# Scores, maxima and masks issued as four products of 32 columns of the array

## The chip, the cores and the metric

The kernel runs on one core of a Trainium2 chip. The metric is device time in microseconds (us) of one execution, lower is better. The engines are named as in the profile: PE is TensorE's products and PEld its weight loads, DVE is VectorE, ACT is ScalarE, POOL is GpSimd, SP is SyncE, which issues DMA transfers.

## The reference

The input is one sequence of 4096 tokens with 256 channels. Four blocks follow one another, each on a layer norm and with a residual sum: a gated recurrence, a feed-forward layer, causal attention with 16 heads of 16 channels, and the feed-forward layer again.

```python
# gated recurrence
i, f, o = (sigmoid(x @ W + b) for W, b in ...); s = tanh(x @ Ws + bs)
h_t = f_t * h_{t-1} + i_t * s_t
y = layernorm(x + o * h) * gamma + beta
# feed-forward
xr = mu_r * x + (1 - mu_r) * x_prev; xk = mu_k * x + (1 - mu_k) * x_prev
out = sigmoid(xr @ W_r.T) * (relu(xk @ W_k.T) ** 2 @ W_v.T)
# attention, in chunks of queries
scores = einsum('bhqd,bhkd->bhqk', q, k) * scale      # -inf where key > query
p = softmax(scores - max(scores)); oc = einsum('bhqk,bhkd->bhqd', p, v)
out = oc @ Wo.T + bo
```

## The kernel before

The layers run in 16 units of 256 tokens. Attention runs in 32 steps: 8 chunks of 512 queries, and for each 4 groups of 4 heads. The heads of a group lie in two pairs. Of each pair one head has rows 0 to 63 of the array and the other rows 64 to 127, `row = HALF * half`, so that two products can run at once, one in each half of the rows. Queries and keys are kept in f16, each in two parts that stand one under the other, and make a stack of 48 rows (`SCORE_ROWS`), or 50 (`STACK`) with two rows that hold the shift by the maximum.

Per step TensorE does this. A maximum ("max", L1751) is a product of up to 512 keys for 128 queries, f16, 48 rows; where its keys reach the diagonal, two products of 64 columns follow in the same half (L1758), bf16, which add the mask. VectorE reduces each to a column (L1539) and frees its PSUM bank. Once a step's maxima are known, VectorE and TensorE form the shift (L1766, f16) and a DMA puts it under the queries. Scores ("scores", L1783) are products of 128 keys for up to 512 queries, f16, 50 rows. ScalarE takes the exponential out of the bank (L1283, or L1294 for two banks at once). P V ("pv", L1804) is four f32 products, one per head, each with 128 rows and 17 columns of the array, side by side in the four groups of 32 columns. Its result is transposed (L1813) and divided.

The layers' products (L1600 in `channels_out`, L1608 in `tokens_out`) are f32 with 128 rows. Each is already issued as four products of 32 columns:

```python
for c in range(0, P, COLUMNS):
    ins = nc.tensor.matmul(bank_chan(b)[c:c + COLUMNS, e], ...
```

Transposes (L1593, L1647, L1813) use all 128 rows and 128 columns.

The order of the work of all engines is written down ahead by `schedule()`, a planner that has costs for each piece of work. It knows three ways in which the array is divided, "half" for maxima, masks and scores, "pv" for P V and the layers' products, "full" for transposes, and counts `SWITCH = 95` ns from one to another. What it gives, `ORDER`, is followed by all engines. Seven PSUM banks go round between maxima, scores and the layers' work, the eighth is P V's. Before TensorE writes a bank again, `claim` waits for the bank's last reader: `span_reduced` for a maximum, `exp_done` for scores.

Of the kernel before, what the change touches and what calls it, by code (L numbers as in the profile page):

```python
# [15 lines left out]
P = 128  # L16
# [23 lines left out]
PAIRS = HG // 2  # L40
# [13 lines left out]
Q_RING = 4  # L54
# [590 lines left out]
def build(nc, x, Wi, bi, Wf, bf, Wo_gate, bo_gate, Ws, bs, gamma, beta, WqT, bq, WkT, bk, WvT, bv, WoT, bo,  # L645
          WrT, WkfT, WvfT, mu_r, mu_k, out):
    with ExitStack() as ctx:
# [95 lines left out]
        def bank(n):  # L743
            return psum[:, n * CHUNK:(n + 1) * CHUNK]
# [836 lines left out]
        def _(pe):  # L1581
# [34 lines left out]
            for op in ORDER:  # L1616
# [69 lines left out]
                elif name in ("q", "kk"):  # L1686
                    _, u, e, b = op
                    if e == 0:
                        claim(b, *((whole_ready[name], u - EARLY + 1) if parts_late(u) else
                                   (part1_ready[name], u + 1)))  # L1690
                        if u == 0:
                            pe.wait_ge(qk_scaled, 1)
                        pe.wait_ge(x3T_ready, u + 1)
                    ins = channels_out(b, weights["aq" if name == "q" else "ak"], a_x3T, e)
                    if e == 1:
                        ins.then_inc(full[name], 1)
                elif name == "v":
                    _, u, j, b = op
                    if j == 0:
                        claim(b, v_ready, u + 1)  # L1700
                        pe.wait_ge(x3T_ready, u + 1)
                    ins = tokens_out(b, weights["av"], a_x3T, j)
                    if j == 1:
                        ins.then_inc(full["v"], 1)
                elif name == "aT":
                    _, u, b = op
                    claim(b, aT_ready, u + 1)
                    pe.wait_ge(attn_ready, GROUPS * (u // 2 + 1))
                    to_channels(b, attn[:, u % 2 * UT:(u % 2 + 1) * UT, :]).then_inc(full["aT"], 1)
                elif name == "proj":  # L1710
                    _, u, j, b = op
                    if j == 0:
                        claim(b, x3_copied if u < UNITS - LATE else x3_ready, u + 1)
                        pe.wait_ge(aT_ready, u + 1)
                    ins = tokens_out(b, weights["ao"], c_columns(u), j)
                    if j == 1:
                        ins.then_inc(full["proj"], 1)
                elif name == "bound":
                    b = op[1]
                    claim(b, bound_read, 1)  # L1720
                    pe.wait_ge(filled, FILLS)
                    pe.wait_ge(prepared, 1)
                    for w in range(2):
                        for k in range(CT):
                            ins = nc.tensor.matmul(bank_tok(b)[:, w], ones, w_squared[:, w, k],
                                                   start=(k == 0), stop=(k == CT - 1))
                    ins.then_inc(full["bound"], 1)
                elif name == "bo":
                    b = op[1]
                    claim(b, bo_ready, 1)  # L1730
                    for k in range(CT):
                        ins = nc.tensor.matmul(bank(b)[:, 0:DIM], bv_cols[:, k], weights["ao"][:, k],
                                               start=(k == 0), stop=(k == CT - 1))
                    ins.then_inc(full["bo"], 1)
                elif name == "max":
                    _, m, half, b = op
                    s, qt, u, k0, k1 = MAXIMA[m]
                    g, c = STEPS[s]
                    maxed += 1
                    claim(b, span_reduced, maxed)  # L1740
                    if s not in q_seen:
                        q_seen.add(s)
                        pe.wait_ge(q_loaded[s % Q_RING], 16 * 2 * len(Q_PARTS) * (s // Q_RING + 1))
                    if c not in k_seen:
                        k_seen.add(c)
                        pe.wait_ge(k_loaded[c % 2], 16 * 2 * len(K_PARTS) * (c // 2 + 1))
                        if c == 0:
                            pe.wait_ge(consts_ready, 4)
                    row = HALF * half
                    ends = k1 == (c * TT + qt + 1) * P  # L1750
                    ins = nc.tensor.matmul(bank(b)[:, 0:k1 - k0],  # L1751
                                           q_stack[row:row + SCORE_ROWS, s % Q_RING, u, qt * P:(qt + 1) * P],
                                           k_stack[row:row + SCORE_ROWS, g * PAIRS + u, k0:k1],
                                           start=True, stop=not ends)
                    if ends:
                        for n in range(2):
                            k = k1 - P - k0 + n * HALF
                            ins = nc.tensor.matmul(bank(b)[:, k:k + HALF], mask_rows[row:row + HALF, n],  # L1758
                                                   mask_keys[row:row + HALF], start=False, stop=(n == 1))
                    ins.then_inc(m_full[half], 1)  # L1760
                elif name == "shift":
                    _, s, b = op
                    claim(b, shift_copied, s + 1)
                    pe.wait_ge(shift_ready, s + 1)
                    for qt in range(TT):
                        ins = nc.tensor.matmul(  # L1766
                            bank(b)[0:HG * MAX_ROWS, qt * P:(qt + 1) * P],
                            shift_parts[:, s % 2, qt * HG:(qt + 1) * HG, :].rearrange("p h r -> p (h r)"),
                            ident_h[:], start=True, stop=True)
                    ins.then_inc(full["shift"], 1)  # L1770
                elif name == "scores":
                    _, tile, i, b = op
                    s, j = TILES[tile]
                    g, c = STEPS[s]
                    q0 = max(0, j - c * TT) * P
                    row, u = HALF * (i % 2), i // 2
                    if j == 0 and scores == HG * tile:
                        pe.wait_ge(shift_placed[s % 2], 16 * HG * (s // 2 + 1))
                        if s == 0:
                            pe.wait_ge(unit_placed, 16 * 2)  # L1780
                    scores += 1
                    claim(b, exp_done, scores)
                    nc.tensor.matmul(bank(b)[:, q0:], k_stack[row:row + STACK, g * PAIRS + u, j * P:(j + 1) * P],  # L1783
                                     q_stack[row:row + STACK, s % Q_RING, u, q0:], start=True, stop=True)\
                        .then_inc(scored[i % 2], 1)
                elif name == "pv":
                    tile = op[1]
                    s, j = TILES[tile]
                    g, c = STEPS[s]
                    d = j - c * TT  # L1790
                    if d >= 0:
                        pe.wait_ge(masked, s * TT + d + 1)
                    else:
                        pe.wait_ge(exp_done, HG * (tile + 1))
                    if j == 0:
                        if s == 0:
                            pe.wait_ge(pv_cleared, 1)
                        else:
                            pe.wait_ge(o_copied, s)
                    if d == 0 and g == 0:  # L1800
                        pe.wait_ge(v_ready, 2 * (c + 1))
                    q0 = max(0, d) * P
                    for h in range(HG):
                        ins = nc.tensor.matmul(pv_bank[32 * h:32 * h + VW, q0:], v_aug[:, j, g * HG + h, :],  # L1804
                                               probs[:, tile % PROBS, h, q0:], start=(j == 0),
                                               stop=(j == TT * (c + 1) - 1))
                    ins.then_inc(pv_done, 1)
                elif name == "out":
                    _, s, b = op
                    claim(b, attn_ready, s + 1)  # L1810
                    pe.wait_ge(o_copied, s + 1)
                    for qt in range(TT):
                        ins = nc.tensor.transpose(bank(b)[:, qt * P:(qt + 1) * P], oT[:, qt * P:(qt + 1) * P],  # L1813
                                                  ident[:])
                    ins.then_inc(full["out"], 1)
# [28 lines left out]
```

## Time and profile before

| | |
|---|---|
| time, median of 2 runs | 1751.32 us |
| the two runs | 1751.12 and 1751.53 us |
| span of the profiled execution | 1749.5 us |
| products on TensorE (as many loads) | 18242 |
| TensorE busy with products | 1709.4 us |
| VectorE busy | 1509.9 us |
| ScalarE busy | 1342.8 us |
| GpSimd busy | 688.8 us |

Both runs lie within 0.5 us of each other; the span of the profiled execution is what the instructions cover, 1.8 us less than the median. A product is booked from its start to its modelled end in PSUM, so that the times of products that follow one another overlap. A weight load (PEld) stands apart from the products that it serves. TensorE's share of busy time therefore says little of short pauses; they are read from the starts.

### The profile page before, as it was taken

The numbers are of one execution on the slowest core, as the hardware profiler recorded it, in microseconds if no ns is written. First come the engines' busy times: TensorE is split into PE (matmuls) and PEld (weight loads), VectorE is DVE, ScalarE is ACT, GpSimd is POOL, SyncE is SP. The second block draws the span as 40 slices with busy tenths as digits, with TensorE's granted clock in tenths as the row PEclk, the third lists the DMA queues.
The fourth block names the chain that finished last, engine by engine and source line by source line (L and its number), as shares of the span: only waits on it lengthen the run. The fifth ranks groups of instructions, "written<-read, shape, count | busy, mean of one in ns | idle before, by whom it ended". The sixth has DMA issues, their size and how long they took to land.

```text
span 1749.5 us, 45658 instructions
## 1 busy us (share of the span) xinstructions
PE 1709.4 (98%) x18242; PEld 641.3 (37%) x18242; DVE 1509.9 (86%) x2975; ACT 1342.8 (77%) x2781; POOL 688.8 (39%) x994
## 2 busy tenths in 40 slices
PE   8999999999999999999999999999999999999997
PEld 6554444344433333334333333332332322222324
DVE  6778979986899999998998999999999999999802
ACT  3336677767677878876888879889889899898894
POOL 3348666478562453428336225220311220212201
PEclk9999999999999999999999999999999999999999
DMA  4132021003002000020000020000002000000000
GB/s 113 56 74 57 27 46 31 18 21 62 28 18 48 13 30 13 8 48 25 6 24 8 21 29 6 24 13 2 7 14 34 18 4 3 14 1 14 2 7 13
DMA packets 57000, 43.71 MB, mean 25 GB/s; under 512 B 8788, under 2 KB 56788, under 8 KB 56788
## 3 DMA queue, kind: packets, MB, share of 16 engines
q1 hardware_dynamic: 54548, 39.75, 9.4%
q8 instruction: 144, 2.36, 0.6%
q10 hardware_dynamic: 2240, 1.05, 0.5%
q14 instruction: 68, 0.56, 0.1%
HBM read 24.00 MB, written 16.25 MB: 23 GB/s over the span
## 4 chain that ended last, share of the span: by engine, by line
PE 60%; DVE 13%; ACT 4%; issue 2%; POOL 2%; SPq 0%; DMA 0%; ACTq 0%; POOLq 0%; DVEq 0%
PE psum L1804 21%; PE psum L1783 12%; PE psum L1751 12%; DVE span_max L1539 12%; PE psum L1608 7%; PE psum L1600 6%; ACT probs L1283 2%; ACT probs L1294 1%; PE psum L1593 1%; PE psum L1813 1%; PE psum L1758 1%; DVE rows L1478 0%; DVE shift_parts L1554 0%; POOL rows L1100 0%; DVE small L1388 0%
## 5 line engine op out<-in xcount | busy, mean ns | idle before, releaser
L1539 DVE TENSOR_REDUCE span_max<-psum 128x1 f32<-128x512 f32 (+3 forms) x2304 | 1313.7, 636 | 98.6 <-PE psum L1751 73.8
L1283 ACT ACTIVATE probs<-psum 128x512 f32<-128x512 f32 (+3 forms) x2148 | 1040.7, 570 | 173.3 <-PE psum L1783 170.1
L1804 PE MATMUL psum<-probs,v_aug 128*17 128x512 f32 (+3 forms) x4608 | 564.9, 562 | 1.3 <-ACT oT L1303 0.8
L1751 PE MATMUL psum<-k_stack,q_stack 48*128 48x512 f16 (+3 forms) x2304 | 533.2, 363 | 4.4 <-DVE span_max L1539 2.7
L1783 PE MATMUL psum<-q_stack,k_stack 50*128 50x512 f16 (+3 forms) x2304 | 521.0, 364 | 5.5 <-DVE span_max L1539 0.7
L1783 PEld LDWEIGHTS psum<-q_stack,k_stack 50*128 50x128 f16 x2304 | 148.7, 93 | 388.7 <-ACT probs L1283 272.4
L1751 PEld LDWEIGHTS psum<-k_stack,q_stack 48*128 48x128 f16 x2304 | 156.0, 93 | 287.9 <-DVE span_max L1539 214.3
L1149 POOL TENSOR_SCALAR_AFFINE_SELECT probs<-probs 128x512 f32<-128x512 f32 x128 | 81.1, 637 | 254.3 <-ACT probs L1283 209.7
L1804 PEld LDWEIGHTS psum<-probs,v_aug 128*17 128x17 f32 x4608 | 77.7, 95 | 136.4 <-issue 114.7
L1188 ACT ACTIVATE rows<-psum,cols 128x256 f32<-128x256 f32 x128 | 53.9, 479 | 56.0 <-PE psum L1600 52.6
L1758 PE MATMUL psum<-mask_keys,mask_rows 64*128 64x64 bf16 x1024 | 93.5, 189 | 0.0
L1142 POOL TENSOR_TENSOR rows<-rows 128x512 f32<-128x512 f32 x26 | 33.1, 1273 | 152.1 <-ACT rows L1225 152.1
L1758 PEld LDWEIGHTS psum<-mask_keys,mask_rows 64*128 64x128 bf16 x1024 | 76.4, 95 | 27.3
L1294 ACT ACTIVATE probs<-psum 128x1024 f32<-128x1024 f32 (+3 forms) x78 | 70.9, 1241 | 3.9 <-PE psum L1783 3.9
L1600 PE MATMUL psum<-rows,w_k 128*32 128x256 f32 x1024 | 68.3, 383 | 3.7 <-DVE rows L1505 2.6
L987 POOL TENSOR_SCALAR rows<-rows,small 128x256 f32<-128x256 f32 x124 | 67.9, 555 | 6.8
L1090 POOL TENSOR_TENSOR rows<-rows 128x512 f32<-128x512 f32 x26 | 27.1, 1041 | 109.9 <-ACT rows L1202 109.9
L1566 DVE RECIPROCAL inv_sum<-psum 128x16 f32<-128x16 f32 x32 | 8.1, 253 | 71.6 <-PE psum L1813 70.9
L1608 PE MATMUL psum<-w_r,rows 128*32 128x256 f32 x1024 | 67.9, 383 | 1.0 <-ACT probs L1283 0.2
L1137 POOL TENSOR_SCALAR rows<-rows 128x512 f32<-128x512 f32 x26 | 16.4, 630 | 131.0 <-ACT rows L1209 130.9
L1388 DVE BATCH_NORM_STATS2 small<-rows 128x6 f32<-128x256 f32 x160 | 59.3, 413 | 9.9 <-POOL rows L1048 3.9
L1608 PE MATMUL psum<-w_v,rows 128*32 128x256 f32 x1024 | 67.4, 383 | 0.4 <-DVE span_max L1539 0.2
(139 smaller groups left out, 1548.1 us busy)
## 6 DMA issues: line engine op xcount, KB each, us to landing
q_stack<-q_parts SPq DMA_DIRECT2D x192, 32.0 KB, 2.0
k_stack<-k_parts SPq DMA_DIRECT2D x42, 128.0 KB, 5.0
rows<-in_x SPq DMA_DIRECT2D x16, 256.0 KB, 2.7
q_parts<-rows SPq DMA_DIRECT2D x32, 128.0 KB, 2.0
k_parts<-rows SPq DMA_DIRECT2D x32, 128.0 KB, 2.0
out<-rows SPq DMA_DIRECT2D x16, 256.0 KB, 2.2
x_rows<-rows SPq DMA_DIRECT2D x14, 256.0 KB, 2.2
rows<-x_rows SPq DMA_DIRECT2D x14, 256.0 KB, 2.7
```

The costliest lines, as they stand in the source:

```text
L987: ins = nc.gpsimd.tensor_scalar(dst[:, j], src[:, j], neg_mean[:, ln, j:j + 1], rstd[:, ln, j:j + 1], ALU.add, ALU.mult)
L1149: nc.gpsimd.affine_select(out=tri, in_=tri, compare_op=ALU.is_ge, fill=0.0, base=0, pattern=[[0, HG], [1, P]], channel_multiplier=-1).then ...
L1283: act.activation(probs[:, tile % PROBS, i, q0:], bank(b)[:, q0:], ACT.Exp, scale=SCALE / QK_SCALE).then_inc(exp_done, 1)
L1294: act.activation(probs[:, tile % PROBS, i:i + 2, q0:], psum[:, b * CHUNK:(b + 2) * CHUNK].rearrange("p (h q) -> p h q", h=2)[:, :, q0:], A ...
L1388: ins = nc.vector.bn_stats(stats[:, ln, j], src[:, j])
L1539: nc.vector.tensor_reduce(span_max[:, s % SPAN_RING, row:row + 1, k0 // SPAN:k0 // SPAN + 1], bank(b)[:, 0:k1 - k0], AX.X, ALU.max).then_i ...
L1600: ins = nc.tensor.matmul(bank_chan(b)[c:c + COLUMNS, e], w[:, k, e * P + c:e * P + c + COLUMNS], src[:, k], start=(k == 0), stop=(k == CT ...
L1608: ins = nc.tensor.matmul(bank_tok(b)[c:c + COLUMNS, j], src[:, k, j * P + c:j * P + c + COLUMNS], w[:, k], start=(k == 0), stop=(k == CT - 1))
L1751: ins = nc.tensor.matmul(bank(b)[:, 0:k1 - k0], q_stack[row:row + SCORE_ROWS, s % Q_RING, u, qt * P:(qt + 1) * P], k_stack[row:row + SCORE ...
L1758: ins = nc.tensor.matmul(bank(b)[:, k:k + HALF], mask_rows[row:row + HALF, n], mask_keys[row:row + HALF], start=False, stop=(n == 1))
L1783: nc.tensor.matmul(bank(b)[:, q0:], k_stack[row:row + STACK, g * PAIRS + u, j * P:(j + 1) * P], q_stack[row:row + STACK, s % Q_RING, u, q0 ...
L1804: ins = nc.tensor.matmul(pv_bank[32 * h:32 * h + VW, q0:], v_aug[:, j, g * HG + h, :], probs[:, tile % PROBS, h, q0:], start=(j == 0), sto ...
```

## The change

Each product of a maximum, of a mask and of scores is issued as four, each for 32 columns of the array and 32 partitions of the bank. Rows, moving operands and results are the same. The wait for the bank stands ahead of the first of the four, and the semaphore is raised by the last. The planner is not touched, so that the order of all work stays.

```diff
-                    ins = nc.tensor.matmul(bank(b)[:, 0:k1 - k0],
-                                           q_stack[row:row + SCORE_ROWS, s % Q_RING, u, qt * P:(qt + 1) * P],
-                                           k_stack[row:row + SCORE_ROWS, g * PAIRS + u, k0:k1],
-                                           start=True, stop=not ends)
+                    for w in range(0, P, COLUMNS):
+                        ins = nc.tensor.matmul(bank(b)[w:w + COLUMNS, 0:k1 - k0],
+                                               q_stack[row:row + SCORE_ROWS, s % Q_RING, u,
+                                                       qt * P + w:qt * P + w + COLUMNS],
+                                               k_stack[row:row + SCORE_ROWS, g * PAIRS + u, k0:k1],
+                                               start=True, stop=not ends)
                     if ends:
                         for n in range(2):
                             k = k1 - P - k0 + n * HALF
-                            ins = nc.tensor.matmul(bank(b)[:, k:k + HALF], mask_rows[row:row + HALF, n],
-                                                   mask_keys[row:row + HALF], start=False, stop=(n == 1))
+                            for w in range(0, P, COLUMNS):
+                                ins = nc.tensor.matmul(bank(b)[w:w + COLUMNS, k:k + HALF],
+                                                       mask_rows[row:row + HALF, n, w:w + COLUMNS],
+                                                       mask_keys[row:row + HALF], start=False, stop=(n == 1))
                     ins.then_inc(m_full[half], 1)
...
-                    nc.tensor.matmul(bank(b)[:, q0:], k_stack[row:row + STACK, g * PAIRS + u, j * P:(j + 1) * P],
-                                     q_stack[row:row + STACK, s % Q_RING, u, q0:], start=True, stop=True)\
-                        .then_inc(scored[i % 2], 1)
+                    for w in range(0, P, COLUMNS):
+                        ins = nc.tensor.matmul(bank(b)[w:w + COLUMNS, q0:],
+                                               k_stack[row:row + STACK, g * PAIRS + u, j * P + w:j * P + w + COLUMNS],
+                                               q_stack[row:row + STACK, s % Q_RING, u, q0:], start=True, stop=True)
+                    ins.then_inc(scored[i % 2], 1)
```

Two places on TensorE show it in the row of instructions. The first is a stretch of maxima (L1751, in the changed kernel L1752), masks (L1758, then L1761) and scores (L1783, then L1788) between two tiles of P V (L1804, then L1810). The shape is columns of the array by columns of the moving operand. Before:

```order
L1804 MATMUL psum<-probs,v_aug 17x512 x4
L1751 MATMUL psum<-k_stack,q_stack 128x512
L1783 MATMUL psum<-q_stack,k_stack 128x512
L1751 MATMUL psum<-k_stack,q_stack 128x256
L1758 MATMUL psum<-mask_keys,mask_rows 128x64 x2
L1751 MATMUL psum<-k_stack,q_stack 128x256
L1758 MATMUL psum<-mask_keys,mask_rows 128x64 x2
L1783 MATMUL psum<-q_stack,k_stack 128x512 x3
L1804 MATMUL psum<-probs,v_aug 17x512 x4
```

The same place after:

```order
L1810 MATMUL psum<-probs,v_aug 17x512 x4
L1752 MATMUL psum<-k_stack,q_stack 32x512 x4
L1788 MATMUL psum<-q_stack,k_stack 32x512 x4
L1752 MATMUL psum<-k_stack,q_stack 32x256 x4
L1761 MATMUL psum<-mask_keys,mask_rows 32x64 x8
L1752 MATMUL psum<-k_stack,q_stack 32x256 x4
L1761 MATMUL psum<-mask_keys,mask_rows 32x64 x8
L1788 MATMUL psum<-q_stack,k_stack 32x512 x12
L1810 MATMUL psum<-probs,v_aug 17x512 x4
```

Nothing changes its place; each row has four times the instructions. The other place is a set of transposes (L1813, then L1819), which takes the array whole, between P V and scores. Before:

```order
L1804 MATMUL psum<-probs,v_aug 17x512 x4
L1813 MATMUL psum<-ident,oT 128x128 x4
L1783 MATMUL psum<-q_stack,k_stack 128x512
L1751 MATMUL psum<-k_stack,q_stack 128x512
L1783 MATMUL psum<-q_stack,k_stack 128x512 x2
```

And after:

```order
L1810 MATMUL psum<-probs,v_aug 17x512 x4
L1819 MATMUL psum<-ident,oT 128x128 x4
L1788 MATMUL psum<-q_stack,k_stack 32x512 x4
L1752 MATMUL psum<-k_stack,q_stack 32x512 x4
L1788 MATMUL psum<-q_stack,k_stack 32x512 x8
```

Between transposes and scores the columns now change with the rows, as they did before between P V and scores. TensorE's products go from 18242 to 35138; the rows of VectorE, ScalarE and SyncE are the same, and so are those of GpSimd but for line numbers.

## Rows read from the trace of the kernel before

**Rows 1.** The page: span, and each engine's busy us (share) and instructions.

```profile
span 1749.5 us, 45658 instructions
...
PE 1709.4 (98%) x18242; PEld 641.3 (37%) x18242; DVE 1509.9 (86%) x2975; ACT 1342.8 (77%) x2781; POOL 688.8 (39%) x994
```

**Rows 2.** Windows of 200 us: length, then each engine's busy us, clock, DMA.

```profile
core 0: us, PE busy (x) PEld busy (x) DVE busy (x) ACT busy (x) POOL busy (x), PEclk, DMA share, GB/s
0.00:200.00 200.00, 186.96 (x2700) 110.64 (x2704) 153.15 (x402) 87.58 (x206) 107.26 (x178) 1.00 0.29 70
200.00:400.00 200.00, 197.74 (x2409) 83.00 (x2403) 165.42 (x352) 143.48 (x321) 127.25 (x184) 1.00 0.12 31
400.00:600.00 200.00, 195.90 (x2206) 76.68 (x2204) 177.90 (x350) 145.59 (x313) 111.77 (x155) 1.00 0.15 31
600.00:800.00 200.00, 198.66 (x2067) 70.34 (x2067) 186.96 (x356) 161.46 (x343) 88.49 (x127) 1.00 0.10 24
800.00:1000.00 200.00, 198.78 (x2122) 71.67 (x2116) 183.22 (x349) 160.25 (x338) 92.75 (x132) 1.00 0.05 16
1000.00:1200.00 200.00, 198.62 (x1903) 64.11 (x1897) 191.60 (x352) 169.72 (x353) 58.66 (x79) 1.00 0.08 17
1200.00:1400.00 200.00, 198.28 (x1853) 60.82 (x1849) 191.82 (x346) 176.47 (x362) 44.37 (x60) 1.00 0.08 16
1400.00:1600.00 200.00, 198.13 (x1731) 58.87 (x1729) 192.39 (x347) 181.09 (x372) 34.19 (x48) 1.00 0.02 6
1600.00:1749.50 149.50, 136.32 (x1285) 45.15 (x1281) 67.39 (x127) 117.19 (x179) 24.10 (x35) 1.00 0.03 8
```

**Rows 3.** The chain of waits, by line, share of the span.

```profile
by line: PE psum L1804 20.6%; PE psum L1783 12.0%; PE psum L1751 11.7%; DVE span_max L1539 11.6%; PE psum L1608 6.7%; PE psum L1600 5.8%; issue 2.4%; ACT probs L1283 2.0%; ACT probs L1294 1.4%; PE psum L1593 1.3%; PE psum L1813 0.7%; PE psu
```

**Rows 4.** Groups by form: count | busy us, mean ns | idle before, releaser.

```profile
L1758 PE MATMUL psum<-mask_keys,mask_rows 64*128 64x64 bf16 x1024 | 93.5, 189 | 0.0
...
L1751 PE MATMUL psum<-k_stack,q_stack 48*128 48x384 f16 x128 | 33.2, 327 | 0.3 <-ACT probs L1283 0.2
...
L1783 PE MATMUL psum<-q_stack,k_stack 50*128 50x384 f16 x128 | 30.5, 328 | 0.5 <-DVE span_max L1539 0.3
...
L1751 PE MATMUL psum<-k_stack,q_stack 48*128 48x256 f16 x128 | 28.8, 275 | 0.4 <-DVE span_max L1539 0.2
...
L1751 PE MATMUL psum<-k_stack,q_stack 48*128 48x128 f16 x128 | 24.0, 222 | 0.5 <-DVE span_max L1539 0.4
```

**Rows 5.** Four lines in short windows: count, duration in ns min/median/max, starts.

```profile
L1608 PE MATMUL psum<-w_r,rows x16: 379/379/403, 1203.0 to 1203.7; 128*32 128x256 f32 x16
...
L1804 PE MATMUL psum<-probs,v_aug x8: 592/598/604, 1207.3 to 1207.7; 128*17 128x512 f32 x8
...
L1751 PE MATMUL psum<-k_stack,q_stack x2: 387/387/387, 1210.2 to 1210.2; 48*128 48x512 f16 x2
...
L1783 PE MATMUL psum<-q_stack,k_stack x3: 376/377/378, 1210.5 to 1210.9; 50*128 50x512 f16 x3
```

**Rows 6.** Timeline of TensorE, 1203 to 1208 us: start us, us, instruction, count.

```profile
1203.03 1.07 PE L1608 MATMUL psum<-w_r,rows 128*32 128x256 f32 x16
1203.91 0.39 PE L1766 MATMUL psum<-ident_h,shift_parts 128*8 128x128 f16 x4
...
1206.05 0.39 PE L1783 MATMUL psum<-q_stack,k_stack 50*128 50x512 f16 x1
1206.05 0.39 PE L1751 MATMUL psum<-k_stack,q_stack 48*128 48x512 f16 x1
1206.54 0.39 PE L1783 MATMUL psum<-q_stack,k_stack 50*128 50x512 f16 x2
1206.76 0.38 PE L1751 MATMUL psum<-k_stack,q_stack 48*128 48x512 f16 x2
1206.98 0.38 PE L1783 MATMUL psum<-q_stack,k_stack 50*128 50x512 f16 x1
1207.29 1.05 PE L1804 MATMUL psum<-probs,v_aug 128*17 128x512 f32 x8
1208.27 0.39 PE L1751 MATMUL psum<-k_stack,q_stack 48*128 48x512 f16 x1
1208.28 0.39 PE L1783 MATMUL psum<-q_stack,k_stack 50*128 50x512 f16 x1
```

**Rows 7.** Timeline of TensorE about two sets of transposes at 649 us.

```profile
648.74 0.66 PE L1813 MATMUL psum<-ident,oT 128*128 128x128 f32 x4
649.23 0.60 PE L1593 MATMUL psum<-ident,rows 128*128 128x128 f32 x4
649.76 0.39 PE L1783 MATMUL psum<-q_stack,k_stack 50*128 50x512 f16 x2
```

**Rows 8.** Timeline: eight weight loads of P V, and four products of L1608.

```profile
1207.29 0.13 PEld L1804 LDWEIGHTS psum<-probs,v_aug 128*17 128x17 f32 x8 [0.43 <-ACT probs L1283]
...
1203.03 0.42 PE L1608 MATMUL psum<-w_r,rows 128*32 128x256 f32 x4
```

## The prediction

> **What bounds the kernel now.** I read the first part of the page, then the busy time of each engine by stretches of 200 us, then the costliest groups, and last the timeline of TensorE. The page gives TensorE 98% of the span, and the granted clock is 1.00, the 2.4 GHz level, in every stretch [rows 1, 2]. But VectorE stands at 183 to 192 us of every 200 from 600 to 1600 us and ScalarE at 160 to 181 [rows 2], and the chain of waits runs 11.6% of the span through the reduction of the maxima [rows 3]. So TensorE leads, with VectorE close behind it in that part.
>
> TensorE's 98% must be read with care. A product of 512 columns of f16 is booked with 377 to 387 ns [rows 5], but two of them, one in each half of the rows, start every 0.22 us: 1206.54, 1206.76, 1206.98 [rows 6]. So 0.16 us of each booking is the tail of the pipeline, and a pause shorter than the tail looks busy. Two kinds of pause hide there. One is a wait for a bank: a pair starts at 1206.05 and the next only at 1206.54 [rows 6]. The other is the switch between ways in which the array is divided. The product at 1206.98 should be through its columns at 1207.20, and P V starts at 1207.29. P V then streams two sets of four products. One set streams for 0.43 us (1.05 us for the eight, less the 0.60 of a single product [rows 5] and 0.02 by which the four of a set start apart), so the columns are through near 1208.17, and the next scores start at 1208.27. Each switch costs some 0.095 us in which nothing streams. Where the division stays, no such gap is there: sixteen products of L1608 at 1203.03 and the four of L1766 at 1203.91 stand 0.88 us apart, which is four sets of 0.216 and the first load [rows 6].
>
> How many switches there are I counted in TensorE's order of instructions: 801 stretches of scores, maxima and masks, 752 entered from P V or a layer's product and 766 left to one; the rest border on transposes. That is 1,518 switches, 144 us, the largest sum that the change could touch.
>
> **The change part by part. The switch.** After the change both sides use 32 columns of the array, but scores still use half the rows and P V all of them. What the trace must answer is whether a change of rows alone costs the gap. It has such a place: a transpose uses all 128 rows and 128 columns, a score half the rows and 128 columns. Eight transposes start at 648.74 and 649.23; the first four take 0.49 us to the next four (4 x 0.107, the rate at which P V streams, plus the first load), the second four 0.53 us to the scores at 649.76, although no load of a transpose lies in this second time [rows 7]. So the change of rows alone shows 0.10 us. I found the same in all places after transposes. I therefore keep the whole 144 us: gain 0. The other bound is the full 144 us, since a transpose may differ from a product in more than its rows; it is rival one. The Trainium skill (TensorEngine Tiling, "Key Properties") says that a change of tiling mode drains TensorE, and lists 64x32 and 128x32 as two modes; by it too nothing is saved here.
>
> **The steady stream.** A pair of 512 columns becomes eight products and eight loads per 0.22 us. Issue isn't the limit: eight loads with the first four products between them go out in 0.13 us less the 0.093 of one load, or 3 to 4 ns an instruction [rows 8], and sixteen need some 55 ns. Nor should the reading be: P V already streams four f32 operands side by side, and four tiles of f16 at twice the columns per us in each half of the rows ask the same bytes of each partition. I take 0, with an upper bound of twice the time (the f32 rate, 0.43 us) in rival two.
>
> **The first load of a stretch.** The first pair after a switch is booked with 387 ns and the later ones with 377: 10 ns of load show. For 128x32 f32 it is 403 against 379, 24 ns; for 128x17 604 against 592, 12 ns [rows 5]. A load of 32 columns is nearest to the 24: + 14 ns for each of 801 stretches, 11 us. Bounds 0 (as the 17 columns) and 41 ns (both halves' loads in turn), 0 to 33 us. The skill ("Gotcha 2: Feature Incompatibilities" on the same page) says that column tiling excludes the fast weight load, which agrees in sign; no run here shows yet that the wide load is a fast one.
>
> **The stagger.** This is the main term. The two products of a pair start within 10 ns. Four narrow ones start 6.7 ns apart: four of L1608 take 0.42 us where one takes 0.403 [rows 5, 8]. Eight then start over 47 ns, and each tile keeps its lag to the end of the stretch, where the switch waits for the last. By my count 479 stretches have an even number of products and end on both halves: + 43 ns; 322 end on one half: + 20 ns. That is 20.6 + 6.4 = 27 us. If products go out at 3.5 ns, it is 13 us. The skill (TensorE: Matmul & The Clock Gate, "The mechanism" in Part 3) gives some 4 ns per tile; by it the term would be 15 us.
>
> **The masks.** 1,024 products of 64 columns stand in 512 groups of two, each now eight. Eight at 6.7 ns are 54 ns, as long as two of 64 columns stream, so one half loses little; the other half's next product waits behind them in order, some 20 ns, in about half of the groups: 5 us, bounds 0 and 20 us.
>
> TensorE's own sum is 11 + 27 + 5 = 43 us, bounds 13 to 85 us.
>
> **How much of it reaches the end.** The order of work is unchanged on all engines. Where TensorE waits for a bank, as at 1206.54, a later TensorE only shortens the wait. At 192 us of 200, VectorE has 8 us of slack per 200 us and TensorE's term is 5 us per 200 us; where the chain runs over VectorE it costs little, elsewhere all. I take six tenths: 26 us. Bounds three tenths of the low sum, 4 us, and all of 43. The profiled execution spans 1749.5 us and the runs took 1751.1 and 1751.5 [rows 1], 1.8 outside it, which stays. Forecast: 1751.3 + 26 = 1777 us, own range 1755 to 1800.
>
> **The rivals.** One: rows don't count, only columns, and the switch to P V is free. For it: no place in the trace changes rows between two real products. Against it: 0.10 us at every change from transposes to scores. TensorE would give back 144 us, 16 us of each 200, but VectorE and ScalarE don't follow. Taking 184 us for the first three stretches, VectorE's busy time with 2% on top for the next five (191, 187, 195, 196, 196) and 137 for the last gives 1,654 [rows 2]; the time would be some 1,660 us, range 1,630 to 1,700.
>
> Two, on the slow side: the narrow loads don't run side by side across the two halves but go in turn. Loads of 27 ns (the 24 ns above) in turn for eight tiles are 0.21 us, just hidden behind 512 columns; from there down they bind. The first pair of each stretch would pay 0.2 us x 801 = 160 us, the narrower products 41 us (L1751 has 128, or 64 pairs, of each of 128, 256 and 384 columns and L1783 as many [rows 4]; 128 pairs each at 0.16, 0.11 and 0.05 us), the 256 pairs of masked products 0.32 us each, 82 us: about 280 us, at nine tenths 2,000 us. In a milder form only the two halves take turns: 27 ns more per stretch, 22 us, and 27 ns more for each of the 1,024 masks, 28 us, which with the 43 makes 93 us on TensorE and at nine tenths 1,835 us. Four loads of a layer's set clearly don't go in turn, since they share the 24 ns; for eight nothing is shown. Half-rate streaming would be worse, 0.22 us x 2,304, over 2,200 us.
>
> Three: the waits take up everything, 1,752 us.
>
> **How the numbers follow.** Forecast 0.60, rival one 0.17, rival two in its milder form 0.10 and in the others 0.05, rival three 0.08. Two per cent, about what a measurement tells from no change, is 35 us: up to 1786. Some three tenths of the forecast's case lies above it. So faster 0.17; slower 0.18 + 0.15 = 0.33; same 0.50. The range leaves out the worst forms of rival two and half of rival one, some 14 in 100 together: 1660 to 1840 us.
>
> **What the profile after would show.** A switch that stays: the last product of a stretch to the first of P V, and back, still 0.09 to 0.10 us after the columns are through, and no load of P V before it. Rival one shows loads of P V inside the stretch of scores. The stagger: eight starts over some 47 ns, and a lag of the same size at the end. The first load: first products booked some 24 ns longer than later ones; rival two shows eight starts or second pairs far later than 0.22 us. VectorE's busy time unchanged. The prediction is wrong if a stretch of three pairs, now 0.8 us from switch to switch, is shorter, or longer by over 0.1 us.

## The result, and the profile after

The changed kernel takes 1765.09 us (1764.61 and 1765.56), against 1751.32 us before: the ratio is 1.0079, with a 95% interval of 1.0049 to 1.0108. It is 13.8 us slower, inside what was forecast and on that side, but about half as much.

The page of the changed kernel, with the queue that fetches instructions:

```profile
span 1763.8 us, 79450 instructions
...
PE 1725.8 (98%) x35138; PEld 676.4 (38%) x35138; DVE 1512.2 (86%) x2975; ACT 1345.0 (76%) x2781; POOL 690.9 (39%) x994
...
q8 instruction: 276, 4.52, 1.1%
```

The span is 14.3 us longer than in [rows 1]. TensorE has 35138 products in place of 18242, VectorE and ScalarE work as long as before, and the fetch of instructions, 2.36 MB before and 4.52 after, holds 0.6% of the transfer engines before and 1.1% after.

The timeline of TensorE at the place of [rows 6], now at 1217 us (start us, us, instruction, count):

```profile
1216.61 0.40 PE L1788 MATMUL psum<-q_stack,k_stack 50*32 50x512 f16 x4
1216.62 0.40 PE L1752 MATMUL psum<-k_stack,q_stack 48*32 48x512 f16 x4
1217.10 0.41 PE L1788 MATMUL psum<-q_stack,k_stack 50*32 50x512 f16 x8
1217.33 0.40 PE L1752 MATMUL psum<-k_stack,q_stack 48*32 48x512 f16 x8
1217.55 0.39 PE L1788 MATMUL psum<-q_stack,k_stack 50*32 50x512 f16 x4
1217.86 1.05 PE L1810 MATMUL psum<-probs,v_aug 128*17 128x512 f32 x8
1218.84 0.40 PE L1752 MATMUL psum<-k_stack,q_stack 48*32 48x512 f16 x4
1218.86 0.40 PE L1788 MATMUL psum<-q_stack,k_stack 50*32 50x512 f16 x4
```

Pairs of four and four still start every 0.22 us: 1217.10, 1217.33, 1217.55. The stream is no slower with eight products in the place of two. Four take 0.40 us where one is booked with 0.387, and eight 0.41: they start some 3.3 ns apart, not 6.7. From the last scores, through their columns at 1217.77, to P V at 1217.86 it is 0.09 us, and from P V back to the maxima 0.98 us as before. So the switch is as dear as it was.

The same two sets of transposes as in [rows 7], in the changed kernel:

```profile
654.92 0.66 PE L1819 MATMUL psum<-ident,oT 128*128 128x128 f32 x4
655.41 0.60 PE L1593 MATMUL psum<-ident,rows 128*128 128x128 f32 x4
655.94 0.41 PE L1788 MATMUL psum<-q_stack,k_stack 50*32 50x512 f16 x8
```

0.49 and 0.53 us, as in [rows 7]. Over the whole trace the gap from the columns' end to the next product is, in the median, 94 ns from scores to P V or a layer, before and after, and 96 ns the other way, where it was 98. In these 752 places a wide product of f16 starts in the median 4 ns after its load and a narrow one 2 ns, which is most of the difference.

The first products after a switch (count, duration in ns min/median/max):

```profile
L1752 PE MATMUL psum<-k_stack,q_stack x4: 386/386/387, 1216.6 to 1216.6; 48*32 48x512 f16 x4
```

They are booked with 386 to 387 ns, as the wide ones are in [rows 5]. The narrow load of f16 shows no more than the wide one.

Two windows of 200 us (length, then PE, PEld, DVE, ACT, POOL busy, clock):

```profile
core 0: us, PE busy (x) PEld busy (x) DVE busy (x) ACT busy (x) POOL busy (x), PEclk, DMA share, GB/s
...
200.00:400.00 200.00, 198.49 (x4464) 86.63 (x4458) 166.80 (x357) 142.02 (x317) 126.18 (x184) 1.00 0.13 31
...
1200.00:1400.00 200.00, 198.41 (x4044) 63.72 (x4028) 190.34 (x344) 175.34 (x359) 42.01 (x58) 1.00 0.08 15
```

VectorE does the same work in more time: it is busy for 190.34 us of these 200, where [rows 2] have 191.82.

Both traces hold the same 1740 stretches between changes of division in the same order, so that they can be laid side by side. From the starts of the products (f16 at 2.4 columns per ns and f32 at 1.2) I summed each kind. The 801 stretches of scores, maxima and masks take 577.2 us before and 595.7 after, 18.5 more. All other stretches change by 0.8 us. The gaps between stretches take 196.3 and 191.5 us, 4.8 less, of which 3 ns x 801 = 2.4 us is the earlier start and the rest shorter waits. An even stretch without masks is longer by 19 ns in the median (285 of them), an odd one by 11 ns (204), an even one with four masks by 23 ns (104). The prediction's own sign of being wrong was a stretch of three pairs that is shorter, or longer by over 0.1 us: the 162 stretches of three full pairs without masks go from 0.663 to 0.683 us in the median, counted from the first start to the end of the columns.

### The profile page after: what moved, and what is told of

Its sections match the earlier page's. It is cut to its first block, busy times and chain, and to the rows that moved or that the text cites. A ratio compares the mean times of both kernels' runs of the same rounds, so it can differ in the third digit from the quotient of the medians.

```text
span 1763.8 us, 79450 instructions
## 1 busy us (share of the span) xinstructions
PE 1725.8 (98%) x35138; PEld 676.4 (38%) x35138; DVE 1512.2 (86%) x2975; ACT 1345.0 (76%) x2781; POOL 690.9 (39%) x994
## 3 DMA queue, kind: packets, MB, share of 16 engines
q8 instruction: 276, 4.52, 1.1%
## 4 chain that ended last, share of the span: by engine, by line
PE 74%; DVE 14%; ACT 4%; POOL 3%; issue 3%; DMA 0%; SPq 0%; ACTq 0%; POOLq 0%; DVEq 0%
PE psum L1810 23%; PE psum L1788 14%; PE psum L1752 14%; DVE span_max L1539 11%; PE psum L1600 9%; PE psum L1608 9%; ACT probs L1283 2%; PE psum L1593 2%; ACT probs L1294 1%; PE psum L1761 1%; PE psum L1819 1%; DVE rows L1478 1%; POOL small L981 0%; POOL rows L987 0%; DVE small L1388 0%
## 5 line engine op out<-in xcount | busy, mean ns | idle before, releaser
L1283 ACT ACTIVATE probs<-psum 128x512 f32<-128x512 f32 (+3 forms) x2148 | 1042.6, 567 | 185.2 <-PE psum L1788 181.9
L1810 PE MATMUL psum<-probs,v_aug 128*17 128x512 f32 (+3 forms) x4608 | 565.0, 562 | 1.3 <-ACT oT L1303 0.8
L1752 PE MATMUL psum<-k_stack,q_stack 48*32 48x512 f16 (+3 forms) x9216 | 548.0, 363 | 3.4 <-DVE span_max L1539 2.4
L1788 PE MATMUL psum<-q_stack,k_stack 50*32 50x512 f16 (+3 forms) x9216 | 536.2, 364 | 5.2 <-DVE span_max L1539 1.0
L1788 PEld LDWEIGHTS psum<-q_stack,k_stack 50*32 50x32 f16 x9216 | 167.2, 89 | 383.0 <-ACT probs L1283 269.4
L1752 PEld LDWEIGHTS psum<-k_stack,q_stack 48*32 48x32 f16 x9216 | 175.5, 89 | 278.1 <-DVE span_max L1539 207.3
L1810 PEld LDWEIGHTS psum<-probs,v_aug 128*17 128x17 f32 x4608 | 77.8, 95 | 138.7 <-issue 115.9
L1761 PE MATMUL psum<-mask_keys,mask_rows 64*32 64x64 bf16 x4096 | 99.0, 189 | 0.2 <-issue 0.2
L1761 PEld LDWEIGHTS psum<-mask_keys,mask_rows 64*32 64x32 bf16 x4096 | 84.9, 94 | 19.9 <-issue 0.3
L1608 PE MATMUL psum<-w_r,rows 128*32 128x256 f32 x1024 | 68.1, 383 | 1.7 <-issue 0.8
L1608 PE MATMUL psum<-w_v,rows 128*32 128x256 f32 x1024 | 67.7, 383 | 0.4 <-DVE span_max L1539 0.2
```

The lines of the kernel that those rows point to most:

```text
L1283: act.activation(probs[:, tile % PROBS, i, q0:], bank(b)[:, q0:], ACT.Exp, scale=SCALE / QK_SCALE).then_inc(exp_done, 1)
L1608: ins = nc.tensor.matmul(bank_tok(b)[c:c + COLUMNS, j], src[:, k, j * P + c:j * P + c + COLUMNS], w[:, k], start=(k == 0), stop=(k == CT - 1))
L1752: ins = nc.tensor.matmul(bank(b)[w:w + COLUMNS, 0:k1 - k0], q_stack[row:row + SCORE_ROWS, s % Q_RING, u, qt * P + w:qt * P + w + COLUMNS], ...
L1761: ins = nc.tensor.matmul(bank(b)[w:w + COLUMNS, k:k + HALF], mask_rows[row:row + HALF, n, w:w + COLUMNS], mask_keys[row:row + HALF], start ...
L1788: ins = nc.tensor.matmul(bank(b)[w:w + COLUMNS, q0:], k_stack[row:row + STACK, g * PAIRS + u, j * P + w:j * P + w + COLUMNS], q_stack[row: ...
```

## The experiments

### One and two: does the gap come with rows, with columns, or with the kind of work?

Only half of the keys of each tile enter P V in these two, so that it takes 64 rows. In the first, all of scores and P V then divide the array alike; in the second (on the kernel before), only the columns differ. Half of P V's sum is left out.

```diff
-  pv_bank[32 * h:32 * h + VW, q0:], v_aug[:, j, g * HG + h, :], probs[:, tile % PROBS, h, q0:]
+  pv_bank[32 * h:32 * h + VW, q0:], v_aug[0:HALF, j, g * HG + h, :], probs[0:HALF, tile % PROBS, h, q0:]
```

> The changed kernel, in which P V's products take only the first 64 of the 128 keys of each tile (rows 0 to 63 of the array, 32 columns), so that half of P V's sum is left out. Scores, maxima, masks and P V then all use 64 rows and 32 columns. Theory (the gap comes with any change in the rows or the columns that a product divides the array into): no gap between scores and P V, and loads of P V inside the stretch of scores; the gaps between P V and the layers' products, which had none, are new. Changes of division fall from 1740 to 753, 987 x 0.095 = 94 us less on TensorE; VectorE holds part of it back: 1,670 to 1,700 us. Rival (the gap comes with any change between f16 and f32 work, or between scores and P V as such): the gap of 0.09 us stays, 1,755 to 1,765 us.

Measured: 1736.8 us, ratio to the kernel before 0.9927 (0.9904 to 0.995), 28 us under the changed kernel. Timeline of TensorE, and below it of the loads:

```profile
1202.07 0.57 PE L1752 MATMUL psum<-k_stack,q_stack 48*32 48x512 f16 x8
1202.28 0.39 PE L1788 MATMUL psum<-q_stack,k_stack 50*32 50x512 f16 x4
1202.50 1.03 PE L1810 MATMUL psum<-probs,v_aug 64*17 64x512 f32 x8
1203.11 0.40 PE L1788 MATMUL psum<-q_stack,k_stack 50*32 50x512 f16 x4
```

```profile
1202.28 0.32 PEld L1810 LDWEIGHTS psum<-probs,v_aug 64*17 64x17 f32 x8
```

P V starts at 1202.50, 0.22 us after the last scores, which is their stream and nothing else, and its loads go out at 1202.28, while those scores run. At 1203.11 scores run in the other half beside P V. In the 747 passages from scores to P V, P V begins in the median 10 ns before all columns of the scores are through, and in eight of ten at most 3 ns after. At the passages from P V to a layer's product, where there was no gap, there is one now, 92 ns in the median (58 of them); both sides are f32 there, and only the rows differ. So it is the division, and neither f16 against f32 nor the kind of work. The time lies above the 1,670 to 1,700 us that I expected. The window of 1200 to 1400 us and the shares of the chain of waits, from the page, point to the reason:

```profile
1200.00:1400.00 200.00, 195.72 (x4116) 73.44 (x4112) 193.51 (x352) 178.14 (x367) 50.02 (x71) 1.00 0.08 18
```

```profile
PE 35%; DVE 30%; ACT 10%; issue 4%; POOL 3%; SPq 0%; DMA 0%; ACTq 0%; POOLq 0%; DVEq 0%
```

VectorE has 193.5 us of 200 and ScalarE 178, and 28% of the span in the chain is the reduction of the maxima, which was 11.6% in [rows 3]. What TensorE gained they didn't follow. A small part is the granted clock, whose mean was 0.988 to 0.996 in the three runs: if TensorE works all the time and the clock is either full or half, a mean of 0.996 costs 0.004 of the span, an estimate of 7 us.

> The kernel before, with the same half of P V's sum left out: scores with 64 rows and 128 columns, P V with 64 rows and 32 columns. Only the columns change between them. Theory (rows or columns): the gap stays, 1802 changes of division in place of 1740, 1,750 to 1,760 us. Rival (rows alone make the gap): as the run before it, under 1,700 us.

Measured: 1774.53 us in the median of five runs, the fastest 1756.95; ratio 1.0098 (1.0059 to 1.0136). Timeline:

```profile
1211.13 0.38 PE L1751 MATMUL psum<-k_stack,q_stack 48*128 48x512 f16 x2
1211.44 1.05 PE L1804 MATMUL psum<-probs,v_aug 64*17 64x512 f32 x8
1212.42 0.39 PE L1783 MATMUL psum<-q_stack,k_stack 50*128 50x512 f16 x1
```

1211.13 + 0.21 to 1211.44: the gap of 0.09 us stays, and back it is 95 ns in the median of 488. Columns alone make it too. The time is over what was expected, for another reason: the granted clock fell in some stretches (see the last section). I ran it again:

> The second experiment's kernel again, since its profiled run fell to a lower granted clock in one stretch. Theory as there: the gap stays, 1,750 to 1,760 us at the full clock.

Measured: 1768.55 us (1760.64 to 1778.46), ratio 1.0103 (1.0063 to 1.0144); the profiled execution, with a mean clock of 0.994, spans 1758.9 us. Above the range again, and with the full clock it was not seen. By the estimate used for experiment one the lost clock is 5 to 32 us in the nine executions of this kernel, and the time without it is 1,747 to 1,753 us in all of them, about that of the kernel before. That the gap stays doesn't hang on the time; it is read from the starts.

### Three: two products of 64 columns

```diff
-                    for w in range(0, P, COLUMNS):
+                    for w in range(0, P, HALF):
```

and in each of the three places slices `w:w + HALF`.

> Scores, maxima and masks as two products of 64 columns. Theory (the added time is the stagger, 3.3 ns for each product after the first, and the order of the masks): 4 starts over 10 ns at the end of an even stretch in place of 23 ns, some 5 us over the kernel before, 1,755 to 1,758 us. Rival (the time comes with the change of the form of the products or of their loads, not with their number): as the changed kernel, 1,765 us. If a load takes its columns at the narrow rate, the first products are booked with 400 ns in place of 387, and 13 ns x 801 = 10 us come on top: 1,766 us.

Measured: 1759.65 us, ratio 1.0046 (1.0033 to 1.006), 8.3 us over the kernel before. The first products after a switch:

```profile
L1752 PE MATMUL psum<-k_stack,q_stack x4: 400/400/400, 1209.5 to 1209.5; 48*64 48x512 f16 x4
```

400 ns in place of 387. So a load of 64 columns shows 13 ns more than one of 32, and also 13 more than the wide one of 128. Half of the expectation fails: the stagger is smaller than in the changed kernel, and the load, which I had put beside it with a question mark, is there. The two don't add to the 1,766 that I wrote: the stagger was only some 3 to 6 ns per stretch, so that the median stretch without masks is 17 to 20 ns longer, 13 of it the load. All 801 stretches together are 10.8 us longer (577.2 to 588.0), less than the medians would give, and the gaps are 1.9 us shorter. Why the sum falls short of the medians I didn't find out.

### Four and five: P V in two halves of the rows, in full

> The kernel before with six PSUM banks in rotation in place of seven and two buffers for rows of x in place of three, for which the planner makes another order. The control for the next run. More waits for banks: 1,760 to 1,800 us.

```diff
-BANKS, PV_BANK = 7, 7
+BANKS, PV_BANK = 6, 7
-X_ROWS = 3
+X_ROWS = 2
```

Measured: 1906.65 us, ratio 1.0888 (1.0871 to 1.0904). Far over what I expected: a bank and a buffer less, and the other order that the planner makes for them, cost 155 us. Which of the two it is was not separated.

> The whole computation, with the banks and buffers of the control. Scores, maxima and masks as in the changed kernel; P V as eight products, four heads with the first 64 keys into one bank and four with the last 64 keys into another, so that all of them use 64 rows and 32 columns. ScalarE copies both banks (some 0.5 us more per step, 16 us), and TensorE adds the two with products with the identity in place of the transposes (128 more of 0.107 us, 14 us). Theory: P V streams as long as before, since both halves run at once, and the gaps between scores and P V go: some 90 us less on TensorE, 14 more, and VectorE holds part of it back, so 40 to 70 us under the control. Rival (the sixteen f32 operands that P V now reads for two halves at once, or the two banks, slow its stream, or VectorE takes all): no less than the control.

```diff
+                    for n in range(2):
+                        rows = slice(HALF * n, HALF * (n + 1))
                         for h in range(HG):
-                            ins = nc.tensor.matmul(pv_bank[32 * h:32 * h + VW, q0:], v_aug[:, j, g * HG + h, :],
+                            ins = nc.tensor.matmul(bank(PV_BANK + n)[32 * h:32 * h + VW, q0:],
+                                                   v_aug[rows, j, g * HG + h, :], ...
```

Measured: 1932.05 us, ratio 1.1039 (1.1021 to 1.1058), 25 us over its control. The rival came true, though not by the means that it named. Timeline:

```profile
1200.82 0.40 PE L1789 MATMUL psum<-q_stack,k_stack 50*32 50x512 f16 x4
1201.04 1.04 PE L1813 MATMUL psum<-probs,v_aug 64*17 64x512 f32 x16
1202.03 0.40 PE L1789 MATMUL psum<-q_stack,k_stack 50*32 50x512 f16 x4
```

Sixteen products of two tiles of P V follow the scores after 0.22 us without a gap and take 1.04 us, as eight did: both halves stream at the full rate. The gap is gone, and the time with it isn't. The shares of the chain of waits, from the page:

```profile
PE 32%; DVE 28%; ACT 8%; POOL 3%; issue 3%; DMA 1%; ACTq 0%; POOLq 0%; DVEq 0%
```

27% of the span in the chain is VectorE's reduction of the maxima, 11% in the control, although VectorE is busy for only 1506 of 1930 us. Before a maximum TensorE sits idle for such a reduction 104 times and 24.0 us in all, against 39 times and 10.6 us in the control, so waits for banks took up at least part of what the gaps gave back. How the 25 us over the control come about I didn't isolate; the other copy by ScalarE and the added products are in it too.

### Six to eight: VectorE made light

VectorE reduces half the columns, so that its part in the 13.8 us, and in what experiment one gained, can be seen. The maximum is then taken over half the keys only.

```diff
-                                            bank(b)[:, 0:k1 - k0], AX.X, ALU.max).then_inc(span_reduced, 1)
+                                            bank(b)[:, 0:(k1 - k0) // 2], AX.X, ALU.max).then_inc(span_reduced, 1)
```

> The kernel before, in which VectorE reduces only the first half of the columns of each maximum, so that the maximum is over half the keys; VectorE's busy time falls by some 600 us. The base for the next two. TensorE's waits for VectorE go: 1,715 to 1,745 us.

Measured: 1726.55 us, ratio 0.9859 (0.9844 to 0.9874).

> The changed kernel with the same half reductions. Theory (TensorE's own term is 16 to 18 us, of which VectorE's waits took a few): 15 to 19 us above the base. Rival (the waits took nothing, and the 13.8 us are all that TensorE loses): 13 to 14 us above the base. Second rival (the added time comes in part by way of VectorE, since its banks come full later): 10 us or less above the base.

Measured: 1741.99 us, ratio 0.995 (0.9933 to 0.9967), 15.4 us over its base. I take that as TensorE's own term. It is 1.6 us over the 13.8, no more than the runs of one kernel lie apart here (1740.6 to 1743.0), so the times alone don't show that waits had swallowed something. The starts of the one profiled execution of each point to it: the stretches of scores are again 18.5 us longer (561.3 to 579.8), but the gaps only 2.9 us shorter, not 4.8.

> The first experiment's kernel (changed kernel, P V over the first 64 of 128 keys) with the same half reductions. Theory (the 987 gaps that are gone are worth 94 us to TensorE, and VectorE was what held them back): 80 us or more under the kernel of the run before it. Rival (ScalarE or the fixed order holds it back as much): within 50 us of it.

Measured: 1680.39 us, ratio 0.9599 (0.9584 to 0.9613), 61.6 us under the run before it. It lies between the theory's 80 and the rival's 50. Window of 1400 to 1600 us:

```profile
1400.00:1600.00 200.00, 195.03 (x4076) 72.14 (x4072) 116.92 (x334) 184.78 (x365) 39.15 (x52) 0.98 0.03 8
```

VectorE is out of the way with 117 us, and ScalarE stands at 185 of 200 in its place. The shares of the chain of waits, from the page:

```profile
PE 59%; ACT 22%; POOL 8%; issue 6%; DVE 2%; DMA 0%; ACTq 0%; POOLq 0%; DVEq 0%
```

The exponentials of ScalarE (L1283) hold 18% of the span, 2.0% in [rows 3]. The mean granted clock of 0.994 to 0.997 takes 5 to 10 us by the estimate used above. With VectorE as it is the same edit gained 28 us, so VectorE held back some 33 us of the 94; some 7 are the clock, and for the other 25 ScalarE and the fixed order are left. I didn't take these two apart.

### Nine and ten: without the masks

```diff
-                    ends = k1 == (c * TT + qt + 1) * P
+                    ends = False
```

> The kernel before without the masks' products (the maxima then see keys past the diagonal). Base for the next: 1,735 to 1,750 us.

Measured: 1746.29 us, ratio 0.9971 (0.996 to 0.9982).

> The changed kernel without the masks' products. Theory (stagger 12 us on TensorE, masks 6): 9 to 12 us above the base, in place of 13.8 with masks. Rival (the masks cost nothing, all is the stagger of the stretches): 13 to 15 us above the base.

Measured: 1754.5 us, ratio 1.0019 (1.001 to 1.0028), 8.2 us over its base, a little under the range of the theory and far from the rival's. By the starts the stretches are 12.4 us longer (568.0 to 580.4) and the gaps 4.5 us shorter. With masks it was 18.5 us: the masks carry 6 us, the stagger 12. This also speaks against a rival that I had not named, the fetch of twice the instructions (2.23 and 4.00 MB in these two): the stagger, worked out from the starts in the next section, is 12.3 us of the 12.4, and little is left for the fetch. With the masks in, nothing was added outside the stretches either.

## Why the prediction was right, and where its sizes were off

**The switch.** Kept at its full 144 us, from the transposes alone. The changed kernel shows it at every passage, experiment one shows it gone once rows and columns agree, and experiment two shows it with the columns alone different. The doubt that a transpose might differ in more than its rows can be dropped. Rival one was false. The Trainium skill (TensorEngine Tiling, "Key Properties") says that a change of tiling mode drains TensorE; the traces agree, with medians of 0.090 to 0.098 us for each change where nothing else is waited for.

**The steady stream.** Taken at 0, measured 0: 0.22 us per pair.

**The first load.** Taken at 14 ns, 11 us in all; it is 0 for 32 columns. The step that failed is the choice of the nearest row: I took 32 columns of f32 as nearest (24 ns). In f16 32 columns show 10 ns (387 less 377) and 64 columns 23 (400 less 377), so columns of f16 show about half the time of those of f32. The range held it, with 0 as its lower end. By the terms of the prediction the upper bound of TensorE's sum is 33 + 27 + 20 = 80 us, not the 85 written there; nothing hangs on it.

**The stagger.** Taken at 6.7 ns per product and 27 us in all; it is 3.3 ns and 12 us. 7 x 3.3 - 4 = 19 ns for even stretches and 3 x 3.3 = 10 for odd ones are what the medians show (19 and 11), and 479 x 0.019 + 322 x 0.010 = 12.3 us. The mistake is the same as with the load: I read the 6.7 ns from products of f32 and used it for f16. It is not the number of rows. P V of experiment two has 64 rows as the scores do, is f32, and follows a switch; four of its products take 0.62 us where one is booked with 0.600, and their starts lie 6.7 ns apart in the median of all its 572 tiles. What is left between them and the scores in these rows is the type of the elements:

```profile
1211.44 0.62 PE L1804 MATMUL psum<-probs,v_aug 64*17 64x512 f32 x4
...
L1804 PE MATMUL psum<-probs,v_aug x4: 600/600/602, 1211.4 to 1211.5; 64*17 64x512 f32 x4
```

The 3.5 ns that I gave as the lower bound was the better value. The Trainium skill (TensorE: Matmul & The Clock Gate, "The mechanism") gives some 4 ns per tile, which was nearer than my row.

**The masks.** Taken at 5 us, shown as 6 on TensorE by the two runs without them.

**What reaches the end.** Taken at six tenths. TensorE's own term with a light VectorE is 15.4 us and 13.8 us arrive, nine tenths. So the slack that I read out of VectorE's 183 to 192 us of 200 took up little. 43 x 0.6 = 26 was forecast. By the starts 18.5 us in the stretches of scores and 0.8 in the others, less 4.8 in the gaps, is 14.5 us, and the spans lie 14.3 apart. The two errors, one of size upward and one of passage downward, partly cancelled, which was luck: the 43 us at nine tenths would have been 39, nearly three times what was measured.

**The rivals.** Two (loads in turn) is excluded by the steady 0.22 us and by the first products' 387 ns. Three (all absorbed) is excluded by the interval.

## What to carry to other kernels

Before equalizing how two kinds of work divide TensorE's array, look whether rows and columns both agree afterwards: each change of either cost 0.09 to 0.10 us here, and a change that equalizes one of the two saves nothing. When a cost is read from the nearest row, take one with the same type of element before one with the same shape: both terms that were mis-sized here came from rows of f32. Splitting a product over groups of columns is nearly free in steady state, but it lengthens each stretch by the lag between first and last start; count the stretches, not the products. And where the gap can be removed, ask first whether the next engine, here VectorE at over 90%, can follow.

## What the runs showed that I had not expected

The granted clock fell with TensorE at work. Windows of experiment two, before, during and after (length, then PE, PEld, DVE, ACT, POOL busy, clock):

```profile
1020.00:1027.00 7.00, 6.56 (x79) 2.42 (x72) 6.58 (x10) 2.93 (x8) 6.83 (x9) 1.00 0.74 84
1027.00:1058.00 31.00, 31.00 (x153) 6.07 (x156) 17.70 (x31) 15.71 (x30) 0.85 (x1) 0.50 0.00 1
1058.00:1065.00 7.00, 7.00 (x67) 1.97 (x60) 6.89 (x12) 5.60 (x12) 0.62 (x1) 1.00 0.01 2
```

For 31 us the clock stood at 0.50, the 1.2 GHz level, while TensorE had products all the time; in the 7 us before, it was booked for 6.56 us and had two idle times of 0.2 us, and P V had half its rows. The profiled executions of the kernels before and after show 1.00 in every window of 200 us, and those of experiments six and seven a mean of 1.0; the other executions of the kernel before have means of 0.997 to 1.0. With a lighter P V or another order of work (one, two, four, five, eight and eleven) the mean is 0.985 to 0.996, in the rest 0.998 to 0.999. What in TensorE's work decides is open.

After a switch products of f16 with 64 rows and 32 columns start every 3.3 ns with their loads, and those of f32 every 6.7 ns, with 128 rows (kernel before) and with 64 (experiment two). Where P V follows scores without a switch, as in experiment one, its loads have gone out before and its four products start 3.7 ns apart in the median of 612 tiles. And products of f32 in eight tiles at once streamed as fast as in four, 0.43 to 0.44 us per 512 columns.
